# Dealing the edge-count groups anew over the units of a graph kernel on one core

## The chip, the cores and the metric

The kernel runs on one core of one Trainium2 chip. The metric is the device time of one execution in microseconds (us), lower is better; times before are the median of three executions. The engines of the core are TensorE (PE in the rows, its weight loads PEld), VectorE (DVE), ScalarE (ACT), GpSimd (POOL) and SyncE (SP, which here issues nearly all transfers).

## What is computed

The reference is one layer of a graph transformer over 1250 nodes with 1024 features and 20000 edges:

```python
xn = layernorm(x)
x = x + gnn(xn, src, dst, ...) + mix(xn)     # two SAGE layers; linear attention
x = x + ffn(layernorm(x))                    # quantized weights and activations, 1024 -> 4096 -> 1024

# one SAGE layer
agg  = segment_sum(h[src], dst)
out  = h @ W_self + (agg / deg) @ W_neigh + b
```

The kernel does not gather rows of `h`. It builds the matrix AT once, with AT[s, m] = number of edges from node s to node m, and multiplies by it in both SAGE layers. The degrees are sums of AT over the sources. This case is about how AT is counted beside other products.

## The kernel before, in words

**Stages around the change.** TensorE works through the stages in a fixed order. Stage U multiplies the attention's q by a folded matrix, ten tiles of 128 nodes (`u_pe`, L2722), 48 products of 512 columns each. The self stage computes `xn @ W_self0`, turned, in UNITS = 12 units (`s0_pe`, L2734): four column blocks times COL_PARTS = 3 parts of the nodes. Units 0, 1, 3, 4, 6, 7, 9 and 10 are long (48 products of 512 columns). Units 2, 5, 8 and 11 are short (48 products of 226 columns, the last nodes). Then stage Z0 computes `xn @ W_neigh0` (`z0_pe`, L2759), and the first product with AT follows (`h_unit`).

**Counting edges.** The edges are sorted by destination. The 1280 padded destinations are cut into NG = 40 groups of 32, and the first is worked on in two parts, so there are 41 parts (here called groups as well). For each chunk of 128 edges VectorE writes two one-hot tiles ("hots"): one of 320 columns at L1827 (the destination within the group and the source's tile) and one of 128 columns at L1829 (the source within its tile). TensorE multiplies them into a bank of PSUM (L2685), and after the group ScalarE copies the bank to AT (L1152, `counts_act`) and zeroes it (L1156). In the self stage a group has two rounds of two chunks each, and so four compares of each kind and four count matmuls; a round is a turn of a loop whose bounds are read from memory, and TensorE waits once for each round's hots (a "pair"). The ring holds eight rounds' hots.

**Where the groups stand.** The list `PARTS` (L62) says how many groups each of the ten tiles of U and each of the twelve units of the self stage takes. TensorE counts them in the midst of a tile's or unit's products, at fixed steps kc of the eight (`counts_between`, L2691): one group at 6, two at 3 and 6, three at 2, 4 and 6. VectorE makes the first group's hots of a tile ahead of the rows of the unit before (`counts_dve`, L1854), and the others behind them:

```python
for t in range(UNITS):
    counts_dve(NT + t, lambda: s0_dve(t))
    s0_split(t)
    ...
    for s in SUMS_AT.get(t, ()):
        source_sum(s)
    if t - 1 in S0_QUADS:
        quad(S0_QUADS[t - 1])
```

`s0_dve` reads the PSUM of the unit before, once it is finished (L1898; in unit 0 it is the last tile of U, L1851 and L1852). `s0_split` (L1545) splits a chunk of the weights of Z0, in the long units. Behind it, unit 0 computes a few scales (`h_scales`, L1879). `source_sum` (L1915) sums AT over the sources for the degrees; `SUMS_AT` (L75) says where four such sums stand. `quad` (L1918) is VectorE's part of a **set**: a piece of the feed-forward weights that is rounded and made into fp8 blocks. ScalarE rounds the set before it (four operations, L1185 and L1189), in unit t if `S0_QUADS` (L457) names t, behind that unit's copies and, in units 0 and 1, behind a mean of other weights (L1162). VectorE does its two operations (L1930, L1933) in unit t + 1. GpSimd then makes the last blocks (L908, L911), and SP stores the set and loads the one after next (L659 to L671). Each engine runs its own instructions in order, and a wait holds up all behind it.

Of the kernel before, what the change touches and what calls it, by code (L numbers as in the profile page):

```python
# [58 lines left out]
QUAD_PARTS = 6  # L59
NB = NG + 1  # L60
LO_UNIT = 256
PARTS = [1] * 4 + [2] * 6 + [2, 2, 1, 3, 2, 1, 3, 3, 1, 3, 3, 1]  # L62
WK, WV, WQ, WO, WN0, WS0, WN1, WS1 = range(8)

NORM_AT = {1: 6 * BANK, 2: 7 * BANK, 3: 2 * BANK, 4: 2 * BANK, 5: 6 * BANK, 6: 6 * BANK}
# [6 lines left out]
LAST_QUADS = 30  # L72
WIDE_QUADS = 16
RING_QUADS = 19
SUMS_AT = {2: (0,), 5: (1,), 8: (2,), 11: (3,)}  # L75
N0_AT = (0, 1, 3, 4, 6, 7, 9, 10)
DEG_AT = 7 * BANK
M_BANK = {0: 6, 1: 6, 2: 6, 3: 6, 4: 6, 5: 2, 6: 4, 7: 6}
# [2 lines left out]
def gps_kernel(nc, x, src_cols, dst_cols, dst_rows, Wself0, Wneigh0, b0, Wself1, Wneigh1, b1,  # L81
               Wq, bq_cols, Wk, bk, Wv, bv, Wo, bo, w_all, w1t, w2t, out):
    ctx = ExitStack()
    with ctx:
# [5 lines left out]
        def S(name):  # L90

            if name not in named:
                named[name] = ctx.enter_context(nc.semaphore(name))
            return named[name]
# [71 lines left out]
        def hot_at(part, q):  # L166

            at_, view = q // 2 * 2 * (GW + P), hots if part >= QUAD_PARTS else quad_hots
            first_s = at_ + 2 * GW + q % 2 * P
            return view[:, :, at_ + q % 2 * GW:at_ + (q % 2 + 1) * GW], view[:, :, first_s:first_s + P]  # L170

        def round_of(part):

            return 2 if part >= QUAD_PARTS else QUAD
# [137 lines left out]
        def alone(eng):  # L312


            eng.sem_inc(S("alone_" + eng.engine.name), 1)
# [11 lines left out]
        def parts_of(tile):  # L327

            return range(sum(PARTS[:tile]), sum(PARTS[:tile + 1]))

# [123 lines left out]
        NPW_all = NPW[:, :, :].rearrange("p w k -> p (w k)")  # L454

        W1_QUADS = 4 * KC // 2
        S0_QUADS = {0: 0, 2: 1, 3: 2, 5: 3, 6: 4, 8: 5, 9: 6}  # L457
        H_QUADS = {0: EARLY_QUADS, 3: EARLY_QUADS + 1, 6: EARLY_QUADS + 2}
        ST_COUNTS = (0, 1, 2, 2, 0, 3, 3, 3, 3, 3)
        ST_QUADS = [range(EDGE_QUADS + sum(ST_COUNTS[:i]), EDGE_QUADS + sum(ST_COUNTS[:i + 1])) for i in range(2 * PAIRS)]  # L460
# [35 lines left out]
        def _(sp):  # L496
# [147 lines left out]
            def quad_store(i):  # L644

                if i < W1_QUADS:
                    to = w1q_parts[:, :, i // 4, i % 4 * BANK // 2:(i % 4 + 1) * BANK // 2]
                else:
                    to = w2q_parts[:, :, i - W1_QUADS, :]
                sp.wait_ge(S("made_last"), 2 * i + 2)  # L650
                sp.dma_start(to, blocks_made(i).rearrange("p s n -> p (s n)").bitcast(F16)
                             .rearrange("p (s n) -> p s n", s=8)).then_inc(S(store_done(i)), 16)
# [6 lines left out]
            for t in range(UNITS):  # L659
                if t in N0_AT[:KC - 2]:  # L660
# [4 lines left out]
                    .then_inc(S(f"rows_out{t % 2}"), 16)  # L665
                if t - 1 in S0_QUADS:
                    i = S0_QUADS[t - 1]
                    quad_store(i)
# [263 lines left out]
        def _(act):  # L932
# [226 lines left out]
            def late_sum(k):  # L1159

                act.wait_ge(S("mean_in"), 16 * k + 16)
                A(TMP[:, 0, :], TMP[:, 0, :], ACT.Abs,  # L1162
                  accum_out=MW_all[:, U_FIRST + k:U_FIRST + k + 1]).then_inc(S("stream_used"), 1)
# [15 lines left out]
            def quad_round(i, part):  # L1179

                w, n = i // W1_QUADS, part % 2
                piece = quad_raw(i)[:, n, :]
                if part < 2:
                    act.wait_ge(pieces_in(i, n), pieces_landed(i, n))
                    A(piece, piece, ACT.Identity, bias=col("magic"), scale=col("isw")[:, w:w + 1])\  # L1185
                        .then_inc(S("rounded"), 2 if i in CLIPPED else 1)
                else:
                    act.wait_ge(S("rounded"), 4 * i + n + 1)
                    A(piece, piece, ACT.Relu, bias=col("to_pos")).then_inc(S("rounded"), 1)  # L1189
# [5 lines left out]
            for t in range(UNITS):  # L1195
# [4 lines left out]
                if NT + t < 2 * HC - U_FIRST:  # L1200
                    late_sum(NT + t)
                if t in S0_QUADS:
                    for part in range(4):
                        quad_round(S0_QUADS[t], part)

# [265 lines left out]
        def _(dve):  # L1471
# [337 lines left out]
            def count_dve(part):  # L1809

                g = max(part - 1, 0)
                dve.reg_load(lohi, bnd[0:1, part:part + 1])
                dve.reg_alu(first, lohi, 8, ALU.logical_shift_right)
                dve.reg_alu(end, lohi, LO_UNIT - 1, ALU.bitwise_and)
                chunks = round_of(part)
                with dve.Fori(dve.snap(first, min_val=0, max_val=EC), dve.snap(end, min_val=1, max_val=EC + 1),
                              chunks) as c_:
                    n = dve.snap(made)
                    dve.reg_alu(slot, made, RING - 1, ALU.bitwise_and)
                    if chunks == QUAD:  # L1820
                        dve.reg_alu(slot, slot, 1, ALU.logical_shift_right)
                    r = dve.snap(slot, min_val=0, max_val=RING * 2 // chunks - 1)
                    dve.wait_ge(S("free"), n + chunks // 2)
                    alone(dve)
                    for j in range(chunks):
                        hot_m, hot_s = hot_at(part, j)
                        V.tensor_scalar(hot_m[:, bass.ds(r, 1), :], iota_m[:, :],  # L1827
                                        key_m[:, bass.ds(c_ + j, 1)], None, ALU.is_equal)
                        one = V.tensor_scalar(hot_s[:, bass.ds(r, 1), :], iota_s[:, :],  # L1829
                                              key_s[:, bass.ds(c_ + j, 1)], -float(g * P), ALU.subtract, ALU.is_equal)  # L1830
                    one.then_inc(S("hot"), chunks // 2)
                    dve.reg_add(made, made, chunks // 2)
# [21 lines left out]
            def counts_dve(tile, between):  # L1854

                parts = list(parts_of(tile))
                count_dve(parts[0])
                between()
                for part in parts[1:]:
                    count_dve(part)  # L1860
# [7 lines left out]
            for t in range(1, NT):  # L1868
                counts_dve(t, lambda: u_dve(t))
# [9 lines left out]
            def h_scales():  # L1879

                dve.wait_ge(S("bq_in"), 48)
                a = col("a_h")
                link(V.tensor_reduce(a, b0s, AXX, ALU.max, apply_absolute_value=True))
                link(V.scalar_tensor_tensor(a, at("p", WS0), 2.0 ** 6, a, ALU.mult, ALU.add))
                link(V.scalar_tensor_tensor(a, at("p", WN0), 2.0 ** 6, a, ALU.mult, ALU.add))
                pow2(a, a)
                ratio(a, a, H_SCALE)
                link(V.tensor_scalar(col("b0"), col("b0"), a, None, ALU.mult))
                times(col("c_h"), at("p", WS0), a, 1.0 / XW)
# [23 lines left out]
            def source_sum(t):  # L1913
                dve.wait_ge(S("at"), 4 * t + 4)
                V.tensor_reduce(deg_part(deg_sums, t), AT_of(t).rearrange("p s n -> p n s"),  # L1915
                                AXX, ALU.add).then_inc(S("added"), 1)
# [19 lines left out]
# [3 lines that stand above are left out]
                if t == 0:  # L1939
                    h_scales()  # L1940
# [5 lines that stand above are left out]
# [511 lines left out]
            for n in range(2):  # L2457
                dve.wait_ge(S("f2_ps"), 7 * p + 7 + n)
                part = slice(BANK + n * BANK // 2, BANK + (n + 1) * BANK // 2)
# [5 lines left out]
        def _(pe):  # L2465
# [225 lines left out]
            def counts_between(tile, more={}):  # L2691

                parts = list(parts_of(tile))
                places = {1: (7 if tile == 0 else 6,), 2: (3, 6), 3: (2, 4, 6)}[len(parts)]

                def at_place(kc):

                    def run():
                        if kc in more:
                            more[kc]()  # L2700
                        return kc in places and count_pe(parts[places.index(kc)])

                    return run

                return {kc: at_place(kc) for kc in {*places, *more}}
# [16 lines left out]
            def u_pe(t):  # L2722
                wait(pe, "u", t - 1)
                product(banks(4 * (t % 2)), lambda l, p: qT[:, l, p, tile_of(t)], of(M_s), 0 if t == 0 else None, "m",
                        counts_between(t, u_first if t == 0 else {}))\
                    .then_inc(S("u_ps"), 1)
# [329 lines left out]
```

## Time and profile before

| | us |
|---|---|
| median of three executions | 1288.04 (1287.69 to 1288.70) |
| profiled execution, own time | 1288.82 |
| its span, first to last instruction | 1287.0 |
| TensorE busy | 1280.6 (100%) |
| VectorE busy | 877.1 (68%) |
| ScalarE busy | 664.2 (52%) |
| GpSimd busy | 96.3 (7%) |
| self stage | 468.44 to 584.45 from the span's start |

Busy shares are over the whole span. Matmuls overlap in their pipeline, so a busy TensorE is not TensorE at its peak; what one product costs is better read from the distance between the starts of many. The chain of waits follows the work that ended last back from the end, and its pieces in order of time tile the span without overlap. In a timeline the durations of neighbours on an engine can overlap a little, so costs are taken between starts.

### The profile page before, as it was taken

Reading aid. Unit: us, or ns where it says so; the run is one execution under the profiler, and the core shown is the slowest. Engines: PE = TensorE matmul, PEld = TensorE weight load, DVE = VectorE, ACT = ScalarE, POOL = GpSimd, SP = SyncE. Lnnn points to the kernel's source line nnn. Section 1 sums busy time; section 2 is a strip of 40 time slices with the busy share of each in tenths; the row PEclk is TensorE's granted clock in tenths of the full one; section 3 lists DMA queues with packets and bytes.
Section 4 is the critical chain, followed back from the end, with each engine's and each line's share of the span. In section 5 each row is a group of like instructions: output and inputs, shape, how many; then the busy total and the mean of one; then the engine's idle time right before and its main releaser. Section 6 shows DMA issues by size and latency. Waiting matters only on the chain.

```text
span 1287.0 us, 19572 instructions
## 1 busy us (share of the span) xinstructions
PE 1280.6 (100%) x6544; PEld 628.5 (49%) x6544; DVE 877.1 (68%) x1529; ACT 664.2 (52%) x938; POOL 96.3 (7%) x91
## 2 busy tenths in 40 slices
PE   9999999999999999999999999999999999999999
PEld 5454445555544445555444554444444444444444
DVE  6954452455567768897992994427877978786674
ACT  7765564556412336443433664547853376565460
POOL 0000000000000001110000100323540000000000
PEclk9999999999999999999999999999999999999999
DMA  9488988566335465645876448599949829732533
GB/s 359 147 266 262 296 256 228 204 230 235 110 115 195 152 209 172 204 139 198 280 249 222 139 131 261 153 353 259 315 133 376 262 74 294 181 68 66 131 61 103
DMA packets 170486, 260.36 MB, mean 202 GB/s; under 512 B 76192, under 2 KB 111776, under 8 KB 166816
## 3 DMA queue, kind: packets, MB, share of 16 engines
q1 hardware_dynamic: 158400, 251.36, 60.1%
q0 software_dynamic: 1440, 5.24, 2.2%
q10 hardware_dynamic: 10560, 2.62, 1.8%
q8 instruction: 52, 0.85, 0.3%
q14 instruction: 34, 0.28, 0.1%
HBM read 184.87 MB, written 57.55 MB: 188 GB/s over the span
## 4 chain that ended last, share of the span: by engine, by line
PE 93%; DMA 2%; DVE 2%; ACT 1%; issue 1%; ACTq 1%; DVEq 0%; SPq 0%
PE ps L2479 26%; PE ps L2839 14%; PE ps L2956 9%; PE ps L2919 9%; PE ps L2744 8%; PE ps L2612 8%; PE ps L2791 7%; PE ps L2809 7%; PE ps L2685 2%; DMA STREAM<-in_w1t 1%; ACTq L958 1%; PE ps L2622 1%; PE ps L2531 1%; PE ps L2513 1%; ACT S L979 1%
## 5 line engine op out<-in xcount | busy, mean ns | idle before, releaser
L2479 PE MATMUL ps<-S,XH 128*128 128x512 f16 x960 | 209.0, 379 | 0.0
L2479 PEld LDWEIGHTS ps<-S,XH 128*128 128x128 f16 x960 | 93.6, 98 | 110.9
L2479 PE MATMUL ps<-S,Zb 128*128 128x512 f16 x480 | 106.7, 379 | 0.0
L2744 PE MATMUL ps<-XH,S 128*128 128x512 f16 (+1 forms) x576 | 105.7, 339 | 0.0
L2612 PE MATMUL ps<-XH,S 128*128 128x512 f16 (+1 forms) x576 | 102.6, 339 | 0.0
L2479 PE MATMUL ps<-Zb,XH 128*128 128x512 f16 x432 | 94.8, 379 | 0.0
L1827 DVE TENSOR_SCALAR STREAM<-tables,keys 128x320 f16 x222 | 67.3, 303 | 34.2 <-issue 17.4
L1152 ACT ACTIVATE AT<-ps 128x320 f16<-128x320 f32 x40 | 17.4, 435 | 139.8 <-PE ps L2479 83.8
L2791 PE MATMUL ps<-XH,AT 128*128 128x512 f16 x400 | 86.7, 379 | 0.0
L2809 PE MATMUL ps<-AT,Zb 128*128 128x512 f16 (+1 forms) x480 | 84.7, 339 | 0.0
L2612 PEld LDWEIGHTS ps<-XH,S 128*128 128x128 f16 x576 | 56.1, 98 | 45.7
L2744 PEld LDWEIGHTS ps<-XH,S 128*128 128x128 f16 x576 | 55.7, 98 | 43.0 <-issue 0.8
L942 ACT ACTIVATE STREAM<-STREAM 128x1024 f32<-128x1024 f32 x64 | 66.8, 1045 | 16.8 <-DMA STREAM<-in_w1t 11.5
L2479 PEld LDWEIGHTS ps<-S,Zb 128*128 128x128 f16 x480 | 46.9, 98 | 54.2 <-issue 0.2
L2839 PE MATMUL ps<-S,XH 128*128 128x512 f16 x300 | 68.8, 379 | 0.0
L2479 PEld LDWEIGHTS ps<-Zb,XH 128*128 128x128 f16 x432 | 42.3, 98 | 50.4 <-issue 0.6
L2809 PEld LDWEIGHTS ps<-AT,Zb 128*128 128x128 f16 x480 | 46.8, 98 | 38.0
L1829 DVE TENSOR_SCALAR STREAM<-tables,keys 128x128 f16 x222 | 64.9, 292 | 0.0
L2791 PEld LDWEIGHTS ps<-XH,AT 128*128 128x128 f16 x400 | 39.1, 98 | 47.3 <-issue 0.3
L1363 ACT ACTIVATE Zb<-ps 128x512 f32<-128x512 f32 x60 | 35.1, 594 | 52.2 <-issue 25.2
L2269 DVE TENSOR_TENSOR Zb<-ps,Zb 128x512 f32<-128x512 f32 x60 | 40.8, 687 | 28.6 <-PE ps L2919 14.4
L1450 ACT ACTIVATE Zb<-Zb,cols 128x1024 f32<-128x1024 f32 x40 | 46.3, 1230 | 23.3 <-DVE cols L2307 23.3
(346 smaller groups left out, 2149.5 us busy)
## 6 DMA issues: line engine op xcount, KB each, us to landing
STREAM<-in_w_all SPq DMA_DIRECT2D x48, 512.0 KB, 5.3
STREAM<-in_w1t SPq DMA_DIRECT2D x42, 512.0 KB, 5.1
STREAM<-in_w2t SPq DMA_DIRECT2D x28, 512.0 KB, 5.7
XIN<-in_x SPq DMA_DIRECT2D x20, 512.0 KB, 5.7
Zb<-in_w1t SPq DMA_DIRECT2D x14, 512.0 KB, 7.4
blocks_scratch<-S SPq DMA_DIRECT2D x4, 1792.0 KB, 8.6
blocks_scratch<-STREAM SPq DMA_DIRECT2D x4, 1792.0 KB, 8.5
S<-blocks_scratch SPq DMA_DIRECT2D x7, 1024.0 KB, 11.3
```

Of the source, the lines that this page charges most:

```text
L942: A(STREAM[:, n % 4, :], STREAM[:, n % 4, :], ACT.Square if n < NORMS else ACT.Abs, accum_out=total).then_inc(S("stream_used"), 1)
L1450: A(piece, piece, ACT.Identity, bias=col("magic"), scale=at("g_sc", t % 2)).then_inc(S("g_magic"), 1)
L1827: V.tensor_scalar(hot_m[:, bass.ds(r, 1), :], iota_m[:, :], key_m[:, bass.ds(c_ + j, 1)], None, ALU.is_equal)
L1829: one = V.tensor_scalar(hot_s[:, bass.ds(r, 1), :], iota_s[:, :], key_s[:, bass.ds(c_ + j, 1)], -float(g * P), ALU.subtract, ALU.is_equal)
L2479: last = mm(acc[:, n * BANK:(n + 1) * BANK], left(l, kc), right(kc, r)[:, n * BANK:(n + 1) * BANK], start=(kc == 0 and i == 0), stop=(kc = ...
L2612: last = mm(ps[:, 3 * j * BANK + a:3 * j * BANK + b], Wq_s[:, kc, l, mc], XH[:, r, kc, a:b], start=(kc == 0 and l == 0 and r == 0), stop=( ...
L2744: last = mm(acc[:, n, :], W[:, kc, r, (c + 4 * n) * P:(c + 4 * n + 1) * P], XH[:, l, kc, unit_cols(u)], start=(kc == 0 and i == 0), stop=( ...
L2791: last = mm(banks(bank + n, 1), AT_tile(t, s), right(r, s, n), start=(s == 0 and r == 0), stop=(s == NT - 1 and r == 1))
L2809: last = mm(acc[:, n, :], Z[:, r, s, (c + 4 * n) * P:(c + 4 * n + 1) * P], AT_cols(u, s), start=(s == 0 and r == 0), stop=(s == NT - 1 and ...
L2839: last = mm(banks(to, 1), left(l, kc), W[:, kc, r, :], start=(start and kc == 0 and n == 0), stop=(stop and kc == KC // 2 - 1 and n == 2), ...
L2919: last = mm(banks(F1_BANKS[s][bank], 1), left[:, kc, :], W1[right][:, kc, j * BANK:(j + 1) * BANK], start=(start and kc == 0), stop=(stop ...
L2956: last = mm(banks(bank, 1), left[:, kc, :], W2[right][:, kc, :], start=(start and kc == 0), stop=(stop and kc == HC // 2 - 1), skip_group_ ...
```

## The change

The two lists are dealt anew, and two places move. `PARTS` puts three groups in U's last tile (two before) and three in each long unit of the self stage, and none in the short units; the total stays 41. `SUMS_AT` moves the first sum from unit 2 to unit 5, where the second already stands. `S0_QUADS` moves ScalarE's rounding of set 0 from unit 0 to unit 1, and so VectorE's and SP's part of it from unit 1 to unit 2. The helpers learn to take a unit without a group.

```diff
-PARTS = [1] * 4 + [2] * 6 + [2, 2, 1, 3, 2, 1, 3, 3, 1, 3, 3, 1]
+PARTS = [1] * 4 + [2] * 5 + [3] + [3, 3, 0] * 4
...
-SUMS_AT = {2: (0,), 5: (1,), 8: (2,), 11: (3,)}
+SUMS_AT = {5: (0, 1), 8: (2,), 11: (3,)}
...
-        S0_QUADS = {0: 0, 2: 1, 3: 2, 5: 3, 6: 4, 8: 5, 9: 6}
+        S0_QUADS = {1: 0, 2: 1, 3: 2, 5: 3, 6: 4, 8: 5, 9: 6}
...
             def counts_dve(tile, between):
 
                 parts = list(parts_of(tile))
-                count_dve(parts[0])
+                for part in parts[:1]:
+                    count_dve(part)
                 between()
                 for part in parts[1:]:
                     count_dve(part)
...
-                places = {1: (7 if tile == 0 else 6,), 2: (3, 6), 3: (2, 4, 6)}[len(parts)]
+                places = {0: (), 1: (7 if tile == 0 else 6,), 2: (3, 6), 3: (2, 4, 6)}[len(parts)]
```

## Rows read from the trace of the kernel before

**Rows 1.** The page's chain by engine; busy times of the self stage (PE, PEld, DVE, ACT, POOL)

```profile
PE 93%; DMA 2%; DVE 2%; ACT 1%; issue 1%; ACTq 1%; DVEq 0%; SPq 0%
...
468.44:584.45 116.01, 116.00 (x676) 65.23 (x674) 103.00 (x247) 58.92 (x88) 15.63 (x14) 1.00 0.56 174
```

**Rows 2.** The chain in order of time, self stage: start us, us, what

```profile
468.44 3.88 PE ps L2744 x18
...
523.76 0.68 PE ps L2685 x4
...
547.11 6.07 PE ps L2744 x48
...
553.89 3.87 PE ps L2744 x24
557.76 0.54 PE ps L2685 x4
...
569.75 0.71 PE ps L2685 x4
570.46 2.71 PE ps L2744 x12
...
584.45 5.61 PE ps L2479 x26
```

**Rows 3.** Timeline of TensorE's weight loads, unit 10's first group, second pair

```profile
569.99 0.25 PEld L2685 LDWEIGHTS ps<-STREAM 128*128 x2 [0.31 <-issue]
```

**Rows 4.** Timeline of ScalarE: the last mean; a copy and two later rounds

```profile
478.24 1.04 ACT L1162 ACTIVATE TMP<-TMP 128x1024 f32<-128x1024 f32 x1
...
554.14 0.44 ACT L1152 ACTIVATE AT<-ps 128x320 f16<-128x320 f32 x1 [6.01 <-PE ps L2744]
...
557.09 2.18 ACT L1189 ACTIVATE Zb<-Zb,cols 128x1024 f32<-128x1024 f32 x2
```

**Rows 5.** Timelines of VectorE and GpSimd, a set and the hots behind it

```profile
563.92 1.22 DVE L1930 TENSOR_SCALAR Zb<-Zb 128x2048 fp8e4<-128x2048 f32 x1
...
566.31 0.30 DVE L1827 TENSOR_SCALAR STREAM<-tables,keys 128x320 f16 x1
566.52 1.09 DVE L1829 TENSOR_SCALAR STREAM<-tables,keys 128x128 f16 x1
...
567.75 1.08 DVE L1829 TENSOR_SCALAR STREAM<-tables,keys 128x128 f16 x1
...
569.35 0.24 DVE L1829 TENSOR_SCALAR STREAM<-tables,keys 128x128 f16 x1
...
566.48 1.09 POOL L908 TENSOR_TENSOR Zb<-Zb 128x512 fp8e4<-128x512 fp8e4 x1 [15.92 <-DVE Zb L1933]
```

**Rows 6.** Timeline of VectorE, unit 0, and two rounds of unit 3

```profile
468.48 1.28 DVE L1851 SCALAR_TENSOR_TENSOR HL<-ps,cols,XIN 128x1024 f32<-128x1024 f32 x1 [3.33 <-PE ps L2479]
...
470.94 0.30 DVE L1827 TENSOR_SCALAR STREAM<-tables,keys 128x320 f16 x1
...
472.21 0.30 DVE L1827 TENSOR_SCALAR STREAM<-tables,keys 128x320 f16 x1 [0.43 <-issue]
...
472.96 1.28 DVE L1545 SCALAR_TENSOR_TENSOR S<-SPLIT,cols,S 128x1024 f16<-128x1024 f32 x1
...
478.19 0.30 DVE L1827 TENSOR_SCALAR STREAM<-tables,keys 128x320 f16 x1 [1.16 <-PE ps L2685]
...
499.83 0.30 DVE L1827 TENSOR_SCALAR STREAM<-tables,keys 128x320 f16 x1 [0.47 <-PE ps L2685]
...
501.65 0.30 DVE L1827 TENSOR_SCALAR STREAM<-tables,keys 128x320 f16 x1 [0.98 <-issue]
```

**Rows 7.** Timeline of VectorE, unit 2: rows, a sum, a group's hots

```profile
492.23 1.52 DVE L1898 TENSOR_SCALAR HL<-ps,cols 128x512 f32<-128x512 f32 x2
493.67 2.33 DVE L1915 TENSOR_REDUCE TMP<-AT 128x128 f32<-128x1280 f16 x1
495.92 0.29 DVE L1827 TENSOR_SCALAR STREAM<-tables,keys 128x320 f16 x1
...
497.26 0.24 DVE L1829 TENSOR_SCALAR STREAM<-tables,keys 128x128 f16 x1
```

## The prediction

> **What bounds the kernel now.** I read the page first, for its chain by engine, then the busy times of the self stage [rows 1]. TensorE stands in 93% of the chain, and in the stage that is changed it is busy for 116.00 of 116.01 us at a granted clock of 1.00, while VectorE is busy for 103.00 of the same 116.01. So time can be taken out only where TensorE does something slower than it must, and it can be put in wherever VectorE delivers late, for its reserve is small. The chain in order of time shows the first of these [rows 2]. Here 18 matmuls of 512 columns take 3.88, so one takes 0.216. In the 6.07 us piece 12 of them stand before 36 short ones (226 columns): (6.07 - 2.59) / 36 = 0.097 for a short one. A group's four count matmuls take 0.54 inside a long unit, but 0.68 inside a short one (0.14 more), and the piece of 12 short and 12 long matmuls after it takes 3.87 where 1.16 + 2.59 = 3.75 are due (0.12 more).
>
> The whole stage, clean, would be 384 x 0.216 + 192 x 0.097 + 98 x 0.135 (count matmuls) = 114.7. It takes 116.0, from 468.44 to 584.45. **So 1.3 us is all that can be won in it**, which is 0.10% of the run; I take 0.2% (2.6 us) as what a measurement can tell from no change. Where the 1.3 lies: some 0.3 in each of units 2, 5 and 8 (the two excesses above), 0.1 in unit 11, and 0.29 in unit 10, which is long: its first group takes 0.71 and the 12 matmuls behind it 2.71 instead of 2.59. That last one is VectorE's lateness, and it gives me the price of any later one, below.
>
> **What the change removes.** No group is left in a short unit, so the 0.3 + 0.3 + 0.3 + 0.1 = 1.0 goes. The number of count matmuls is the same. The group moved into U's last tile costs 0.54 there and is 0.54 less in the self stage: nothing. There, VectorE makes the hots for the third group in the 3.33 us in which it waited for U's end [rows 6], and TensorE wants them 9 us into the tile; covered. ScalarE's copies move with their groups and it idles for several us before most of them; covered. On SP's queue the store of set 0 and the load of set 2 come one step later, behind the store of unit 2's rows; ScalarE wants set 2 only after unit 3's third count, so this hides, and if it does not, the rounding of set 2 is late, which VectorE reaches only well into unit 4.
>
> **What the change moves onto VectorE's order.** Its program is fixed: in each unit the first group's hots, the rows of the unit before (which wait for that unit's end), the other groups, the split, sums, a set. So I ask, unit by unit, when the second pair of hots of a group is finished and when it is due. T0 is the start of unit 0. A long unit with three groups is 48 x 0.216 + 3 x 0.54 = 11.98; its groups end at 3.13, 6.26 and 9.39. A short one without a group is 4.64.
>
> The price of lateness comes from unit 10: the second pair of hots is finished at 569.35 + 0.24 = 569.59 [rows 5], its weights load at 569.99 (0.40 later) [rows 3], the next product starts at 570.46 (0.47 later) and loses another 0.12 [rows 2]. So a late group ends 0.40 + 0.47 + 0.12 = 0.99 after its second pair; here at 570.58, against 570.29 due. That is the 0.29. From below, the pair could be taken up at once and end after its own two matmuls, 0.27; I take 0.99, the only row in which it happened.
>
> *Unit 3, the largest.* Set 0 now stands in unit 2. ScalarE rounds it behind unit 1's third count and the last mean. That count ends at T2 - 2.59. The copy starts 0.25 later (553.89 to 554.14) [rows 2, 4]; from there to the end of four rounds it is 557.09 + 2.18 - 554.14 = 5.13, and the last mean adds 1.04 [rows 4]: finished at T2 + 3.83. VectorE's two operations of the set take 2.39 (563.92 to 566.31), so the hots of unit 3's first group start at T2 + 6.22 [rows 5]. Right then GpSimd works on the same set (from 566.48), and the first two 128-column compares take 1.09 and 1.08 where a later one takes 0.24: the second pair is finished 569.59 - 566.31 = 3.28 after the start, at T2 + 9.50 [rows 5]. The group ends at T2 + 10.49. It is due at 4.64 + 3.13 = 7.77. **Stall: 2.7 us**, from below 2.0. Before, a group inside unit 2 and the set's later place kept these apart.
>
> Of that overlap the Trainium skill (SBUF — State Buffer, Who interferes with whom) says that VectorE and GpSimd take one port pair in turn, each for a whole instruction, and the other blocks fully. By the rule alone the hots could lose all of GpSimd's two operations, 2.2 us, where the rows show 3.28 lasting against 1.58 without it (495.92 to 497.26 + 0.24) [rows 7], 1.70 lost; the sum would be 0.5 higher.
>
> *Unit 1.* In unit 0, VectorE's second group starts its two rounds 2.50 and 3.77 after T0 (470.94 and 472.21). A further group, new here, follows 1.82 later (as 501.65 after 499.83) and 1.3 after that, at 5.6 and 6.9 [rows 6], and ends 0.75 after its second round starts, at 7.65. The split, the scales and the restart take 472.96 to 478.19 = 5.23, so unit 1's first group starts at 12.9, its second round at 14.2, finished 0.8 later at 15.0, and the group ends at 16.0 against 11.98 + 3.13 = 15.11. Stall 0.9, from below 0.2; its later groups follow closely, and I add 0.1: 1.0.
>
> *Unit 6.* In unit 5 VectorE now has the rows (1.44) and two sums (2.25 each) before it can start unit 6's hots: T5 + 5.94; second pair 1.58 later, 7.52 [rows 7]; the group ends at 8.51, due 7.77. Stall 0.75, from below nothing.
>
> *Units 4 and 10.* Each follows a long unit with three groups and a set, the pattern in which unit 10 lost 0.29. Unit 4 follows the late unit 3: 0 to 0.4, I take 0.2. Before unit 10 VectorE now meets unit 8 without a group and comes some 0.5 earlier: 0 to 0.3, I take 0.1. Unit 7 has more room, since its predecessor starts late with VectorE back in step: nothing. In units 8 and 11 one sum (T + 3.7) leaves the next hots or rows in time: nothing.
>
> **Sum.** 2.7 + 1.0 + 0.75 + 0.2 + 0.1 = 4.75 added, 1.0 + 0.29 = 1.3 removed: **+3.5 us**. After the stage nothing absorbs it: its last piece and the first product behind it are back to back in the chain, so the rest shifts. The profiled execution took 1288.82 around a span of 1287.0, and the three runs have a median of 1288.04; the difference goes onto the median: 1291.5.
>
> **Rivals.**
> - *TensorE takes late hots up at once* (the 0.27 end of each price): 2.0 + 0.3 + 0.1 - 1.3 = +1.1, 1289.1, not slower by what can be told. For it: 0.40 was seen once. Against it: the one late group of this profile was not taken up so. With prices half way it gives 1290.3. Chance 0.23.
> - *VectorE stays ahead, and only the gain is left.* This needs unit 3's second pair by about T2 + 6.8, so set 0 rounded 2.7 us earlier than ScalarE's order allows by my count. Then -1.3, 1286.7, the faster side of no change. The same time comes out if the sequence of sets is in effect the old one. Chance 0.08.
> - *Lateness is handed on*: VectorE does not regain step after unit 3, and each of the next sets hits the next first group (units 4, 6, 7, 10 at 0.5 to 0.7 more each): +6, 1294. For it: VectorE at 103.00 of 116.01. Against it: the other 13 us are left to regain step. Chance 0.12.
> - *The clock falls after the stall.* Every row shows 1.00, but none has a wait of 2.7 us in it. If the rest of unit 3 (36 matmuls, 7.8) ran at the lower of the two levels, 1.2 instead of 2.4 GHz, it would cost 7.8 more, 1299. The Trainium skill (TensorE: Matmul & The Clock Gate, What's actually happening) has an idle engine put back to the lower level. No row bears this out. Chance 0.02.
> - My forecast: 0.55, by itself 1290.3 to 1292.7.
>
> **The numbers.** Slower by over 0.2% (above 1290.6) holds most of the forecast, the third and fourth rival: 0.65. Within 0.2%: the first two rivals and the low edge of the forecast, 0.33. Faster by over 0.2% would need twice the whole idle excess: 0.02. The range reaches from the first rival's price to the near edge of the third: 1289.0 to 1293.5.
>
> **What would show it.** Right: in the chain of the changed kernel the short units are single pieces of 4.64 us; the self stage takes about 119 us (116.0 less the moved group's 0.54, plus 3.5); the longest gap of TensorE stands before unit 3's first group, with VectorE's compares of over 1 us directly ahead; small ones in units 1 and 6. Wrong: no gap in unit 3, or the set's two operations in unit 2 starting before T2 + 2; or gaps in the stages behind the self stage.

## The result, and the profile after

The changed kernel takes 1292.87 us (median of six, 1292.51 to 1293.73) against 1287.87 for the kernel before (also six runs, 1287.65 to 1288.70): **+5.0 us**, ratio 1.0037, 95% interval [1.0026, 1.0047]. The forecast was +3.5, slower by over 0.2%, between 1289.0 and 1293.5; 1292.87 lies within that range.

The first view is the busy times of the self stage and of the stage behind it (start:end, length, then PE, PEld, DVE, ACT, POOL; the column of 1.00 is the granted clock). The second is the largest entry among the waits of TensorE in the whole span (us in total, how many, the longest).

```profile
468.66:588.75 120.09, 116.29 (x671) 64.67 (x670) 97.25 (x239) 58.36 (x86) 15.50 (x14) 1.00 0.54 170
588.75:692.90 104.15, 104.15 (x503) 47.62 (x502) 82.81 (x77) 38.30 (x33) 0.00 (x0) 1.00 0.72 238
```

```profile
PE ps L2686 <- DVE STREAM L1829: 3.8, 5, 1.7
```

The stage was 116.01 long with TensorE busy for 116.00 of it [rows 1]. Now it is 120.09 with 3.8 us of idle time, all of it before count matmuls (L2686, which was L2685) and all of it ended by VectorE's hots. With the 0.54 of the group that moved ahead of the stage, that is 4.62 us more. What comes behind it is as long as it was: from the stage's end to the span's end 1291.3 - 588.75 = 702.55, before 1287.0 - 584.45 = 702.55. So the whole loss is made in the self stage, at five groups.

(The two profiled spans differ by 4.3, and not 4.6, because the changed kernel's stage began only 0.22 later (468.66 for 468.44) where the moved group makes 0.54 due; the last section has more on this.)

The timeline of TensorE shows the five. A first group in a long unit costs 2.59 (12 products) and 0.54; distances between the starts of the products tell where more was paid.

```profile
477.89 5.34 PE L2745 MATMUL ps<-XH,S 128*128 128x512 f16 x24
483.07 0.44 PE L2686 MATMUL ps<-STREAM 128*128 x2
484.14 0.52 PE L2686 MATMUL ps<-STREAM 128*128 x2 [0.63 <-DVE STREAM L1829]
484.61 2.76 PE L2745 MATMUL ps<-XH,S 128*128 128x512 f16 x12
487.20 0.44 PE L2686 MATMUL ps<-STREAM 128*128 x2
488.03 0.47 PE L2686 MATMUL ps<-STREAM 128*128 x2 [0.39 <-DVE STREAM L1829]
488.45 2.76 PE L2745 MATMUL ps<-XH,S 128*128 128x512 f16 x12
491.05 0.71 PE L2686 MATMUL ps<-STREAM 128*128 x4
491.64 9.99 PE L2745 MATMUL ps<-XH,S 128*128 128x512 f16 x72
503.36 0.46 PE L2686 MATMUL ps<-STREAM 128*128 x2 [1.73 <-DVE STREAM L1829]
504.32 0.52 PE L2686 MATMUL ps<-STREAM 128*128 x2 [0.50 <-DVE STREAM L1829]
504.79 2.76 PE L2745 MATMUL ps<-XH,S 128*128 128x512 f16 x12
...
511.06 5.34 PE L2745 MATMUL ps<-XH,S 128*128 128x512 f16 x24
516.24 0.94 PE L2686 MATMUL ps<-STREAM 128*128 x4
517.14 2.76 PE L2745 MATMUL ps<-XH,S 128*128 128x512 f16 x12
...
523.41 9.99 PE L2745 MATMUL ps<-XH,S 128*128 128x512 f16 x72
533.36 0.46 PE L2686 MATMUL ps<-STREAM 128*128 x2
534.33 0.46 PE L2686 MATMUL ps<-STREAM 128*128 x2 [0.50 <-DVE STREAM L1829]
534.74 2.76 PE L2745 MATMUL ps<-XH,S 128*128 128x512 f16 x12
...
553.00 9.98 PE L2745 MATMUL ps<-XH,S 128*128 128x512 f16 x72
562.83 0.71 PE L2686 MATMUL ps<-STREAM 128*128 x4
```

Ahead of a first group stand either 24 long products (5.18) or 12 long, 48 short and 12 long ones: the chain of the changed kernel has the last such piece as 9.82 (`553.17 9.82 PE ps L2745 x72`), and 553.00 to 562.83 agrees, so a short unit without a group is clean, 9.82 - 5.18 = 4.64. With 0.54 for the group the due distances are 5.72 and 10.36, and behind a second group 3.13. Read:

| group | distance of starts | due | late |
|---|---|---|---|
| unit 1, first | 484.61 - 477.89 = 6.72 | 5.72 | 1.00 |
| unit 1, second | 488.45 - 484.61 = 3.84 | 3.13 | 0.71 |
| unit 3, first | 504.79 - 491.64 = 13.15 | 10.36 | 2.79 |
| unit 4, first | 517.14 - 511.06 = 6.08 | 5.72 | 0.36 |
| unit 6, first | 534.74 - 523.41 = 11.33 | 10.36 | 0.97 |

Together 5.8 us, and with 0.06 behind unit 1's third group 5.9. The 1.3 us that could be won [rows 1, 2] were won: no group in a short unit any more, and unit 10's first group in time. 5.9 - 1.3 = 4.6.

What VectorE and GpSimd did ahead of unit 3 is in their timelines:

```profile
498.25 1.23 DVE L1931 TENSOR_SCALAR Zb<-Zb 128x2048 fp8e4<-128x2048 f32 x1 [2.29 <-ACT Zb L1189]
499.52 1.23 DVE L1934 TENSOR_TENSOR Zb<-Zb 128x1024 fp8e4<-128x1024 fp8e4 x1
500.66 0.30 DVE L1827 TENSOR_SCALAR STREAM<-tables,keys 128x320 f16 x1
500.87 1.10 DVE L1829 TENSOR_SCALAR STREAM<-tables,keys 128x128 f16 x1
...
502.11 1.08 DVE L1829 TENSOR_SCALAR STREAM<-tables,keys 128x128 f16 x1
...
503.70 0.24 DVE L1829 TENSOR_SCALAR STREAM<-tables,keys 128x128 f16 x1
...
500.83 1.10 POOL L908 TENSOR_TENSOR Zb<-Zb 128x512 fp8e4<-128x512 fp8e4 x1 [217.78 <-DVE Zb L1934]
```

VectorE had idled 2.29 us for ScalarE's rounding of set 0. It then did its two operations of the set, and behind them the hots, the first two 128-column compares at the slow pace of [rows 5], while GpSimd worked on the set from 500.83 on. Unit 2 begins at 494.39 (the 72 products began at 491.64, and their pipeline runs 0.16 ahead; 12 x 0.216 later). The set starts 3.86 into it (forecast 3.83) and the second pair is finished 9.55 into it (forecast 9.50).

### The profile page after: what moved, and what is told of

It is laid out like the page before. It is cut to its first block, busy times and chain, and to the rows that moved or that the text cites. A ratio compares the mean times of both kernels' runs of the same rounds, so it can differ in the third digit from the quotient of the medians.

```text
span 1291.3 us, 19572 instructions
## 1 busy us (share of the span) xinstructions
PE 1282.0 (99%) x6544; PEld 628.2 (49%) x6544; DVE 873.5 (68%) x1529; ACT 664.9 (51%) x938; POOL 97.0 (8%) x91
## 4 chain that ended last, share of the span: by engine, by line
PE 84%; DVE 4%; DMA 4%; issue 3%; ACT 2%; ACTq 1%; DVEq 1%; SPq 0%
PE ps L2480 25%; PE ps L2840 14%; PE ps L2920 9%; PE ps L2613 8%; PE ps L2957 7%; PE ps L2792 7%; PE ps L2810 7%; PE ps L2745 4%; PE ps L2686 2%; DMA STREAM<-in_w1t 2%; ACTq L958 1%; DMA STREAM<-in_w_all 1%; PE ps L2623 1%; DMA S<-HL 1%; PE ps L2514 1%
## 5 line engine op out<-in xcount | busy, mean ns | idle before, releaser
L2745 PE MATMUL ps<-XH,S 128*128 128x512 f16 (+1 forms) x576 | 105.6, 340 | 0.0
L1827 DVE TENSOR_SCALAR STREAM<-tables,keys 128x320 f16 x222 | 65.8, 297 | 39.1 <-issue 20.9
L2745 PEld LDWEIGHTS ps<-XH,S 128*128 128x128 f16 x576 | 55.5, 98 | 42.3 <-issue 1.1
L1829 DVE TENSOR_SCALAR STREAM<-tables,keys 128x128 f16 x222 | 61.4, 277 | 0.0
```

What stands on the lines that cost most here:

```text
L1827: V.tensor_scalar(hot_m[:, bass.ds(r, 1), :], iota_m[:, :], key_m[:, bass.ds(c_ + j, 1)], None, ALU.is_equal)
L2745: last = mm(acc[:, n, :], W[:, kc, r, (c + 4 * n) * P:(c + 4 * n + 1) * P], XH[:, l, kc, unit_cols(u)], start=(kc == 0 and i == 0), stop=( ...
```

## Experiments

Two theories. **Lateness**: TensorE pays only where VectorE's fixed order delivers a group late, and each of the five late groups has a cause of its own: unit 0's third group ahead of the scales (unit 1), the moved set (units 3 and 4), the moved sum (unit 6). **The dealing itself**: three groups in a long unit are more than the unit can take, whatever stands around them. The experiments undo the parts of the change one by one, or do one alone. "Stage" below is the distance from the first product of unit 0 to the first of Z0 in the timeline (before: 116.0, changed: 120.1); "run" is the difference of medians to the kernel before, measured beside it (median 1288.31 beside e1 to e4, 1288.40 beside e5 to e8). Each kernel ran 10 or 11 times, e2 and e8 five times. The intervals are about 1.2 us to either side, 1.8 for e2 and e8.

| kernel | stage | run | ratio, 95% interval |
|---|---|---|---|
| e1: changed, set 0 back | 117.0 | +1.9 | 1.0016 [1.0007, 1.0025] |
| e2: changed, GpSimd held back on set 0 | 119.9 | +4.9 | 1.0036 [1.0022, 1.0050] |
| e3: changed, set 0 and sum 0 back | 116.0 | +0.7 | 1.0001 [0.9992, 1.0010] |
| e4: before, set 0 moved | 118.5 | +2.6 | 1.0018 [1.0009, 1.0027] |
| e5: e3, unit 0 two groups, one more in U | 113.7 | -0.6 | 0.9997 [0.9988, 1.0006] |
| e6: e3, unit 0 two groups, unit 2 one | 114.9 | -0.7 | 0.9995 [0.9986, 1.0004] |
| e7: before, sum 0 moved | 116.1 | +0.3 | 1.0002 [0.9993, 1.0011] |
| e8: changed, sum 0 back | 119.2 | +4.2 | 1.0035 [1.0022, 1.0048] |

**e1, the set back.**

```diff
-        S0_QUADS = {1: 0, 2: 1, 3: 2, 5: 3, 6: 4, 8: 5, 9: 6}
+        S0_QUADS = {0: 0, 2: 1, 3: 2, 5: 3, 6: 4, 8: 5, 9: 6}
```

> The changed kernel with set 0 back where it was (rounded in unit 0, VectorE's part in unit 1). Lateness theory: the stall before unit 3's first group (2.80 us in the changed kernel's trace) and the 0.36 in unit 4 that follows from it go; unit 1's 1.8 and unit 6's 1.0 stay. So the self stage 3.1 us shorter (about 117.0) and the whole run about 1.9 us above the kernel before. Rival, the dealing itself costs (three groups in a long unit): within 1 us of the changed kernel, +4 to +5.

Measured: stage 117.0, run +1.9. In TensorE's timeline unit 3's first group is whole again,

```profile
491.69 9.99 PE L2745 MATMUL ps<-XH,S 128*128 128x512 f16 x72
501.51 0.71 PE L2686 MATMUL ps<-STREAM 128*128 x4
502.06 2.75 PE L2745 MATMUL ps<-XH,S 128*128 128x512 f16 x12
```

502.06 - 491.69 = 10.37, as due. Unit 4 is in time as well, and units 1 and 6 are as late as in the changed kernel, within 0.1 (three waits, 1.6 us). So 3.1 of the 4.6 us belong to the moved set, and the dealing itself is ruled out as the main cause.

**e4, the set alone.** The same line in the kernel before, the other way round.

> The kernel before with one edit, set 0 moved to units 1 and 2. Lateness theory: unit 3's first group ends 10.5 us after unit 2's start and is due at 5.51 + 3.13 = 8.64, since unit 2 here holds a group and lasts longer: a stall of 1.9 us and nothing else, the run +1.9 us. Rival, the dealing itself costs and the set does not: 0.

Measured: stage 118.5, run +2.6: unit 3's first group is 2.1 late for the expected 1.9, with two waits of 1.08 and 0.50, and small excesses, in units 7 and 10 above all, make up the other 0.4 of the stage. The set costs this in the old dealing too; it costs less there because unit 2 holds a group and lasts longer.

**e8, e3 and e7, the sum.** Alone back in the changed kernel (e8), back together with the set (e3), and alone moved in the kernel before (e7):

```diff
-SUMS_AT = {5: (0, 1), 8: (2,), 11: (3,)}
+SUMS_AT = {2: (0,), 5: (1,), 8: (2,), 11: (3,)}
```

> The changed kernel with the first sum back in unit 2, where VectorE waits for ScalarE's rounding of set 0 anyway (2.3 us idle). Lateness theory: unit 6's 0.98 goes and unit 3's 2.80 stays as it is (the sum ends as the rounding ends, at most 0.2 later): self stage about 119.1, the run 4.0 us above the kernel before. Rival, sum and set add up in unit 2: unit 3's stall grows by up to 2.3, +6.

> The new dealing alone: set 0 and the first sum both back. Lateness theory: besides unit 3 and 4, unit 6's 1.0 goes, unit 1's 1.8 stays, the short units are clean pieces of 4.64: self stage about 116.0, the run about 0.9 us above the kernel before. Rival, the dealing itself costs: +4 to +5.

> The kernel before with one edit, the first sum moved to unit 5. Lateness theory: unit 5 here holds a group and lasts 0.87 us longer, so unit 6's first group, which ends about 8.6 after unit 5's start, is due at 8.6: no stall or up to 0.3, the run as the kernel before. Rival, a second sum in unit 5 costs what it cost in the changed kernel: +1.0.

e8: stage 119.2, run +4.2. Unit 6's lateness is gone and unit 3's is as it was (a wait of 1.74 where the changed kernel has 1.73): the sum fits into the time in which VectorE waits for ScalarE. e3: stage 116.0, run +0.7, which its interval does not tell from nothing; what is left of TensorE's waits in the stage is unit 1's:

```profile
PE ps L2686 <- DVE STREAM L1829: 1.1, 2, 0.7
```

e7: stage 116.1, no difference that can be told. Unit 6's first group is 0.32 later than before, and unit 10's is in time where it was 0.29 late. By the stages, the moved sum thus costs 1 us only together with the new dealing, which takes the group, and 0.9 us, out of unit 5.

**e5 and e6, unit 0.** Both build on e3:

```diff
-PARTS = [1] * 4 + [2] * 5 + [3] + [3, 3, 0] * 4
+PARTS = [1] * 4 + [2] * 4 + [3] * 2 + [2, 3, 0] + [3, 3, 0] * 3    # e5
+PARTS = [1] * 4 + [2] * 5 + [3] + [2, 3, 1] + [3, 3, 0] * 3        # e6
```

> The new dealing with set 0 and the first sum back, and one group moved out of unit 0 into the last but one tile of U: unit 0 two, every other long unit three, short units none. Lateness theory: unit 1's 1.8 us goes, since VectorE reaches its scales one group earlier; the self stage is clean, 12 units with 22 groups, (116.04 - 1.8 - 0.54) = 113.7 us, the run about 1.2 us below the kernel before. It could lose up to 1 us in U, where VectorE must make the last but one tile's third group (three rounds) behind a split. Rival: unit 1 is late because of U's third group in the last tile, or through the dealing as such: its 1.8 us stays.

> As the one before, but the group out of unit 0 goes into unit 2, a short one, and U stays as in the changed kernel. Lateness theory: unit 1's 1.8 us goes and about 0.33 us (the excess of a group inside a short unit) comes back: self stage 116.04 - 1.8 + 0.3 = 114.6, the run about 0.8 us below the kernel before. Rival as before: 1.8 us stays.

(The stage of e5 holds 23 groups, not 22 as the expectation has it; the changed kernel's holds 24. The 0.54 for one group is right.) e5: stage 113.7 as expected. TensorE waits for no group at all; its waits in the whole span are

```profile
PE ps L2566 <- POOL squares L878: 1.2, 1, 1.2
PE ps L2920 <- DVE Zb L2270: 0.3, 1, 0.3
PE ps L2920 <- ACT Zb L1363: 0.2, 1, 0.2
```

Its last tile of U still has three groups, so unit 1 was late through unit 0's third group and not through U's. That this group delays unit 1 by pushing back the split and the scales is read from VectorE's order; no run moved the scales. U lost some 0.5 us: its last but one and last tiles have groups that take 3.54 and 3.49 from product to product where 3.40 and 3.13 are due. The run is 0.6 us below the kernel before. e6: stage 114.9, run -0.7; unit 1 is in time, and the group in unit 2 costs its excess of 0.3 there and another 0.4 at unit 3's first group. Both intervals hold 1, so neither is shown to be faster than the kernel before. Both are faster than the changed kernel: their slowest runs took 1289.49 and 1288.75, its fastest 1292.51.

**e2, GpSimd's part.** In GpSimd's `last_blocks`:

```diff
                 pool.wait_ge(S("made"), 2 * i + 2)
+                if i == 0:
+                    pool.wait_ge(S("s0"), 6)
```

> The changed kernel, with GpSimd held back on set 0 until VectorE has written unit 2's rows, that is, until unit 3's first hots are written. Overlap theory: these hots are finished 1.7 us earlier, 1.6 instead of 3.3 after their start, and the stall in unit 3 falls from 2.8 to about 1.1; the run about 3.2 us above the kernel before. Rival, the compares behind a set are slow for a reason of VectorE's own: the two compares of 1.1 us stay, and the time is the changed kernel's, +5.

The mechanism came as expected, the time did not. VectorE's and GpSimd's timelines (this kernel has two lines more, so its L1829 and L1831 are L1827 and L1829 of the others):

```profile
502.58 0.25 DVE L1831 TENSOR_SCALAR STREAM<-tables,keys 128x128 f16 x1
...
503.66 0.30 DVE L1829 TENSOR_SCALAR STREAM<-tables,keys 128x320 f16 x1 [0.46 <-issue]
...
505.65 1.10 DVE L1829 TENSOR_SCALAR STREAM<-tables,keys 128x320 f16 x1 [0.26 <-issue]
...
506.83 1.13 DVE L1829 TENSOR_SCALAR STREAM<-tables,keys 128x320 f16 x1
...
505.55 1.10 POOL L910 TENSOR_TENSOR Zb<-Zb 128x512 fp8e4<-128x512 fp8e4 x1 [221.39 <-DVE HL L1901]
```

The compare right behind the set takes 0.25 instead of 1.10, and the compares that now run beside GpSimd take 1.10 and 1.13: the slowness goes where GpSimd goes. The Trainium skill (SBUF — State Buffer, Who interferes with whom) has the two take one port pair in turn where VectorE's instruction is in a two-port mode, which tensor_scalar can enter, or reads two SBUF inputs. This agrees with it, though no row tells the mode. The first group's lateness fell by 1.40, from 2.79 to 505.10 - 493.35 - 10.36 = 1.39, for the 1.7 expected. Its hots were finished only 1.14 earlier (2.14 after their start, for 3.28), for without the slow compares VectorE's second round starts 1.29 after the first and no longer follows at once. But the second group, which now meets GpSimd, is late by 509.73 - 505.10 - 3.13 = 1.50, and this is why the time hardly moved: the wait was handed on within the unit.

## Why the prediction was right, point by point

**The side, the place and the cause held; the size was short.** The measured 1292.87 lies in the stated range, but above the 1290.3 to 1292.7 that the forecast's own mechanism was given: the edge up to 1293.5 came from the third rival. The stage took 120.1 where about 119 was forecast. TensorE's chain is broken by VectorE at the first groups of units 3, 1, 6 and 4, in this order of size, and nothing behind the stage changed. e1, e3 and e5 take the causes out one after the other: 120.1, 117.0, 116.0, 113.7 (the last step also moves a group, 0.54, out of the stage).

- *Removed, 1.3*: right. Short units take 4.64, and unit 10 is in time (forecast 0.1 late). The later store and load of the sets hid, too: ScalarE waited 3.0 us for loads in the stage (0.5 before), but VectorE waited for ScalarE only once, at set 0.
- *Unit 3, 2.7*: measured 2.79, by the forecast's own steps, the set at T2 + 3.86 for 3.83. The hots took 3.28 again; the 0.5 more that the port rule taken alone would give did not come. (Where the forecast has "the set's later place" before, the set stood a unit earlier, in unit 1.)
- *The price of a late group, 0.99 after its second pair*: 2.79 + 7.77 - 9.55 = 1.01 in unit 3. It is made in another way than was told, though: TensorE picks up awaited hots after 0.16, not 0.40, and the rest goes into its loop (last section). Where only the second pair was waited for, in unit 1's first group, the price was less: finished at 483.98, the group's end at 484.61 + 0.16, so 0.79.
- *Unit 6, 0.75*: measured 0.97. In the changed kernel VectorE finishes set 2 only at 526.31, 0.15 after unit 5's start, and its two sums take 4.62 for 4.50.
- *Unit 4, 0.2*: measured 0.36, within its 0 to 0.4.
- *Unit 1, 1.0*: measured 1.77, the term that was sized wrong. The first group is 1.00 late for 0.9, and that is near by luck: its second pair was finished 15.33 after T0 (483.98 after 468.49 + 0.16) for the 15.0 forecast, and the price was 0.79 for 0.99. The step that failed is "its later groups follow closely, and I add 0.1". The second group's second round did not follow the first at once:

```profile
485.37 0.29 DVE L1827 TENSOR_SCALAR STREAM<-tables,keys 128x320 f16 x1
...
486.95 0.30 DVE L1827 TENSOR_SCALAR STREAM<-tables,keys 128x320 f16 x1 [0.67 <-issue]
```

It started 1.58 later, and why it took so long is not shown. Its hots were finished at 487.87 where the first group's lateness had made them due at 487.6 or so (an estimate, 0.27 before the group's due end), and the slow restart of TensorE was paid a second time: 0.71.

The sum's error of 4.6 - 3.5 = 1.1 is thus unit 1's 0.8, 0.2 each for units 4 and 6 and 0.1 for unit 3, less 0.1 for unit 10; the remaining 0.4 of the measured +5.0 is not explained by the stage and is of the size by which the three medians of the kernel before differ (1287.87 to 1288.40).

**The rivals.** Hots taken up at once (+1.1) is out by its price: they are in fact picked up after 0.16, but no late group cost as little as 0.27 after its second pair. That only the gain is left is out for the change, and came half true for e5. Unit 3 handed its lateness on only to unit 4 (0.36); units 7 and 10 are in time. The clock stayed at 1.00 in the stage, with a wait of 1.73 in it. The fall to the lower level that the Trainium skill (TensorE: Matmul & The Clock Gate, What's actually happening) describes for an idle engine was not seen.

## What to carry to other kernels

When an in-order engine feeds a bound engine just in time, count for each delivery when it is finished and when it is due, and let the order of its other work decide, not the busy share: VectorE was less busy in the changed stage (97.3 of 120.1 us, for 103.0 of 116.0) and delivered later. Shortening the consumer's work (here a short unit by its group) also moves every deadline behind it forward, so a piece of work that was free in that unit stops being free. And a block of work beside which a third engine contends should not stand directly ahead of a delivery: moving the block back took 3.1 us off the stage (e1), and moving the third engine alone 0.2 (e2).

## What the hardware showed beyond that

- **A stalled loop restarts slowly on TensorE.** Weight loads follow the finished hots by 0.16 when TensorE stands waiting: 484.14 after 483.73 + 0.25, and 503.35 after 502.11 + 1.08. But behind the first round's load in units 3 and 6, which both came late, the second round's comes 0.96 later, though in unit 3 its hots (503.94) were finished 0.37 before it. In the timelines of VectorE and of TensorE's weight loads:

```profile
483.73 0.25 DVE L1829 TENSOR_SCALAR STREAM<-tables,keys 128x128 f16 x1
...
503.35 0.25 PEld L2686 LDWEIGHTS ps<-STREAM 128*128 x2 [2.22 <-issue]
504.31 0.30 PEld L2686 LDWEIGHTS ps<-STREAM 128*128 x2 [0.71 <-issue]
504.78 2.27 PEld L2745 LDWEIGHTS ps<-XH,S 128*128 128x128 f16 x12 [0.16 <-issue]
```

  In a unit that runs ahead, all four loads of a group take 0.58. So a late group costs more than the idle time that the profile shows for it: 1.00, 0.71, 2.79 and 0.97 late with 0.63, 0.39, 2.23 and 0.50 idle, which leaves 0.3 to 0.6, and unit 4's is 0.36 late with none. I take the loop's own instructions between the rounds for it, hidden when the engine runs ahead; this was not tested.
- **The same holds on VectorE**: rounds follow each other by 0.75 at best (504.70 and 505.45, at unit 3's second group, where VectorE came late and had not idled) and by 1.3 or more elsewhere (1.29 in e2's first group of unit 3; 1.31 and 1.58 in unit 1). What decides between the two was not tested apart. So slow compares cost less than their excess: without them the hots were finished 1.14 earlier in e2, where 1.70 was expected.
- **Single profiles differ ahead of the stage.** The stage's start moved by up to 2.0 us between kernels that are alike up to there (467.68 in e7 and 469.73 in e4, with U as before; 468.18 in e8 and 470.14 in e2, with U as changed). TensorE's waits for VectorE far ahead of the stage differ too: none in e7, 1.8 us in e4 (L2531). The self stage by itself repeats better: unit 1's first group is 1.00 to 1.03 late in the changed kernel, e1 and e3. The intervals of whole runs reach 1.2 us to either side at best.
